# Expert blocks in another order: where the helpers' work for the next block stands, in a one-core Trainium2 kernel

## The chip, the core and the metric

The kernel runs on one core of a Trainium2 chip. The core has five engines with instruction streams of their own, which wait for each other through semaphores: TensorE (PE) multiplies matrices, VectorE (DVE) and ScalarE (ACT) work elementwise and can read TensorE's results in PSUM, GpSimd (POOL) works elementwise and issues gathers and scatters, SyncE (SP) issues other DMAs. The metric is the device time of one execution in microseconds; the figure for the kernel is the median of three runs.

## What is computed

Six sublayers stand one after another, each of the form x = x + f(layernorm(x)): cross attention, self attention, a feed-forward layer, cross attention again, a recurrent memory, and a mixture of experts. x is 16 x 64 x 256 in float32, the context 16 x 1601 x 192. The change touches the last sublayer alone (1024 tokens of width 256, eight experts, the two best for each token, and a shared expert for all):

```
logits = normed @ router_w.T;  probs = softmax(logits)
top_v, top_i = top_k(probs, 2);  gates = softmax(top_v)
for e in range(8):
    gate, up = split(normed @ gate_up_w[e].T)      # 256 -> 2 x 768
    y = (silu(gate) * up) @ down_w[e].T            # 768 -> 256
    out = out + comb[:, e, None] * y
out = out + swiglu(normed, shared_gate_up_w, shared_down_w)
```

## The kernel before

The program is a list of functions for each sublayer, one per engine, called one after another; what an engine does stands in the order of the calls in the code. In `moe` (L2525) the routing first sorts the 2048 pairs of token and expert into `NS` = 23 blocks of 128 rows, each of one expert. `itu` and `itd` hold, for each block, the offset of its expert's weights in the SBUF tensors `gu` and `dn`.
For block i the work is this:

- GpSimd gathers 128 rows (`gather`, three ahead) into `xs`.
- TensorE transposes them (`turn_block`, two transposes on L166, PSUM bank 6), VectorE scales and shifts them into `XT` (`take_block`, L2773).
- ScalarE rounds `XT` to fp32r as the high part `Xh` (`block_high`, L2947), GpSimd subtracts it to get the low part `Xl` (`block_low`, L3010).
- The expert's gate/up weights come in three thirds f = 0, 1, 2 of 1024 columns in all. ScalarE rounds each to its high part `hi[f]` (`up_high`, L2953), VectorE makes the low part `lo[f]` (`up_low`, L2783).
- TensorE makes the product of each third in PSUM bank f (`gate_up`): four matmuls with the high weights (L2666, L2667), two with the low ones (L2670). Block 0 alone uses float32 weights directly (L2660).
- ScalarE applies silu to one half of the product (L2939), VectorE multiplies it with the other (L2789) into `a_`.
- TensorE transposes the six 128-column pieces of `a_` (`turn_a`, six transposes on L166), ScalarE copies them to SBUF in two copies (L2961), and TensorE makes the down product from them (`down`, L2692; each of its six float32 matmuls appears as two).
- VectorE scales the result by the gates (L2795) and GpSimd adds it to the output rows in HBM (`add`, L3017).

The loop is software pipelined. In the round of block i TensorE does the products of block i, the turns and the down product of block i-1, and the transposes of a later block's input. The weights' parts for block i+1 are made meanwhile, a third at a time, each behind the product of block i that frees its buffer. Every engine works in order, so an instruction that waits holds all that are queued behind it on that engine.

The register load for the down product (L2686) stands on TensorE ahead of all waits of `down`; ScalarE's (L2981) at the start of a round; VectorE's (L2782) in `up_low`, behind its wait for the high part.

Of the kernel before, what the change touches and what calls it, by code (L numbers as in the profile page):

```python
# [16 lines left out]
NS = 23  # L17
# [2507 lines left out]
def moe(c, m, ended, tail):  # L2525
# [32 lines left out]
    ids, itu, itd = m.irest[:, 0:NS], m.irest[0:1, NS:2 * NS], m.irest[0:1, 2 * NS:3 * NS]  # L2558
# [9 lines left out]
    routed, routing, prob = c.sig("routed"), c.sig("routing"), c.sig("prob")  # L2568
# [35 lines left out]
    def pe(e, w):  # L2604
# [36 lines left out]
        def turn_block(i):  # L2641
            w.wait_ge(*in_xs[i % 3](i))
            w.wait_ge(*emptied[6])
            for k in range(2):
                p = c.turn(e, ps[:, 6, 128 * k:128 * k + 128], xs[i % 3][:, 128 * k:128 * k + 128])
            p.then_inc(b_turned.at(i), 1)
            emptied[6] = b_taken(i)

        off = {}
# [33 lines left out]

        def down(i):
            bank = (5, 7)[i % 2]
            off[i, 1] = e.value_load(itd[:, i:i + 1], min_val=0, max_val=7 * 1536)  # L2686
            for part in range(2):
                w.wait_ge(*a_taken((i, 3 + part)))
                w.wait_ge(*in_dn(7))
                w.wait_ge(*emptied[bank])  # L2690
                for f in range(4 * part, 4 + 2 * part):
                    p = e.matmul(ps[:, bank, 0:256], aT[i % 2][:, f, :], dn[:, bass.ds(off[i, 1] + 256 * f, 256)],  # L2692
                                 start=(f == 0), stop=(f == 5))
            p.then_inc(y_made.at(i), 1)
            emptied[bank] = y_out(i)
# [29 lines left out]
            emptied[b] = s  # L2725
        turn_block(0)
        for i in range(NS):
            gate_up(i, 0)
            gate_up(i, 1)
            if i:  # L2730
                turn_a(i - 1)
            else:
                turn_block(1)
            gate_up(i, 2)
            if i + 2 < NS:
                turn_block(i + 2)
            if i:
                down(i - 1)
        turn_a(NS - 1)
# [2 lines left out]
    def dve(e, w):  # L2742
# [34 lines left out]
        off = {}  # L2777

        def up_low(i, f):
            w.wait_ge(*up_hi((i, f)))  # L2780
            if f == 0:
                off[i] = e.value_load(itu[:, i:i + 1], min_val=0, max_val=7 * 3072)  # L2782
            e.tensor_tensor(lo[f], gu[:, bass.ds(off[i] + 1024 * f, 1024)], hi[f], ALU.subtract).then_inc(up_lo.at((i, f)), 1)  # L2783

        def gate_up(i, f):
            w.wait_ge(*silu((i, f)))
            w.wait_ge(*(a_turned((i - 2, 4)) if i >= 2 else sh_down(NT - 1)))
            w.wait_ge(*routed("table"))
            e.tensor_tensor(a_[i % 2][:, 256 * f:256 * f + 256], ps[:, f, 256:512], sg[f], ALU.mult).then_inc(a_made.at((i, f)), 1)  # L2789
# [116 lines left out]
        shared_down(1)  # L2906
        take_block(0)
        for i in range(NS):
            gate_up(i, 0)
            gate_up(i, 1)  # L2910
            if i == 0:
                take_block(1)
            if i + 1 < NS:
                up_low(i + 1, 0)
            gate_up(i, 2)
            if i + 2 < NS:
                take_block(i + 2)
            if i + 1 < NS:
                up_low(i + 1, 1)
            if i:  # L2920
                down(i - 1)
            if i + 1 < NS:
                up_low(i + 1, 2)
        down(NS - 1)

    def act(e, w):
        def shared_act(half, f):
            w.wait_ge(*sh_up((half, f)))
            if half:
                w.wait_ge(*sh_act((half - 1, f)))  # L2930
            e.activation(sgs[f], ps[:, sh_bank(half, f), :], ACT.Silu).then_inc(sh_silu.at((half, f)), 1)

        def gate_up(i, f):
            w.wait_ge(*g_made((i, f)))
            if i:
                w.wait_ge(*a_made((i - 1, f)))
            else:
                w.wait_ge(*sh_down(NT - 1))
            e.activation(sg[f], ps[:, f, 0:256], ACT.Silu).then_inc(silu.at((i, f)), 1)  # L2939

        off = {}

        def block_high(i):
            w.wait_ge(*b_taken(i))
            if i >= 3:
                w.wait_ge(*g_made((i - 2, 2)))
            e.copy(Xh[i % 2], XT[i % 2]).then_inc(x_hi.at(i), 1)  # L2947

        def up_high(i, f):
            if i == 1:  # L2950
                w.wait_ge(*(h_out("h"), routing("down"), sum_out(1))[f])
            w.wait_ge(*g_made((i - 1, f)))
            e.copy(hi[f], gu[:, bass.ds(off[i] + 1024 * f, 1024)]).then_inc(up_hi.at((i, f)), 1)  # L2953

        def turn_a(i):
            for n, b in ((4, 3), (2, 4)):
                f0 = 0 if b == 3 else 4
                w.wait_ge(*a_turned((i, b)))
                if i >= 2:
                    w.wait_ge(*y_made(i - 2))  # L2960
                e.copy(flat(aT[i % 2][:, f0:f0 + n, :]), ps[:, b, 0:128 * n]).then_inc(a_taken.at((i, b)), 1)  # L2961

        e.activation(c.sd[:, 0:1], c.ident[:, 0:1], ACT.Sqrt).then_inc(c.ac.at(), 1)
        tail.take_rows(e, w, LT - 2, 6, 256)
        tail.take_rows(e, w, LT - 1, 6, 0)
        w.wait_ge(*c.dv(("moments", into, LT)))
        w.wait_ge(*c.po("eps"))
        e.activation(c.sd[:, LT:NT], c.mv[:, LT, 1:2], ACT.Sqrt, bias=c.eps).then_inc(c.root.at(into), 1)
        e.activation(c.sd[:, 1:2], c.ident[:, 0:1], ACT.Exp).then_inc(c.ac.at(), 1)
        ended(w)  # L2970
        w.wait_ge(*routing("logits"))
        e.activation(pr, lg, ACT.Exp).then_inc(prob.at("in"), 1)
        w.wait_ge(*routing("gap"))
        e.activation(g2, v2, ACT.Exp).then_inc(prob.at("gate"), 1)
        for half in range(2):
            for f in range(2):
                shared_act(half, f)
        w.wait_ge(*routing("down"))
        for i in range(NS):
            if i + 1 < NS:  # L2980
                off[i + 1] = e.value_load(itu[:, i + 1:i + 2], min_val=0, max_val=7 * 3072)  # L2981
            gate_up(i, 0)
            gate_up(i, 1)
            if i:
                turn_a(i - 1)
            else:
                block_high(1)
            if i + 1 < NS:
                up_high(i + 1, 0)
            gate_up(i, 2)  # L2990
            if i + 1 < NS:
                up_high(i + 1, 1)
            if i + 2 < NS:
                block_high(i + 2)
            if i + 1 < NS:
                up_high(i + 1, 2)
        turn_a(NS - 1)

    def pool(e, w):
        def gather(i):  # L3000
            w.wait_ge(*routing("ids"))
            w.wait_ge(*h_out("h"))
            if i >= 3:
                w.wait_ge(*b_turned(i - 3))
            e.indirect_dma_start(xs[i % 3], None, c.xs_d, bass.IndirectOffsetOnAxis(ap=ids[:, i:i + 1].bitcast(U32), axis=0)
                                 ).then_inc(in_xs[i % 3].at(i, 16), 16)

        def block_low(i):
            w.wait_ge(*x_hi(i))
            e.tensor_tensor(Xl[i % 2], XT[i % 2], Xh[i % 2], ALU.subtract).then_inc(x_lo.at(i), 1)  # L3010

        def add(i):
            w.wait_ge(*y_out(i))
            w.wait_ge(*sum_out(1))
            if i:
                w.wait_ge(*added(i - 1))
            e.indirect_dma_start(rows_out, bass.IndirectOffsetOnAxis(ap=ids[:, i:i + 1].bitcast(U32), axis=0), yS[i % 2], None,  # L3017
                                 bounds_check=1023, oob_is_err=False, compute_op=ALU.add).then_inc(added.at(i, 16), 16)

        root_pool(c, e, w, into, LT - 1)  # L3020
        ended(w)
        e.memset(C_[:, :, NS:NS + 1], 0.0).then_inc(c.po.at("past the last"), 1)
        w.wait_ge(*routing("placed"))
        w.wait_ge(*c.dv("gates"))
        ce = cmp_[:, 0:16 * NS].rearrange("p (i s) -> p i s", s=NS)
        e.tensor_tensor(B[:, :, NS:2 * NS], ce, g12.unsqueeze(2).broadcast_to([128, 16, NS]), ALU.mult).then_inc(gated.at("in"), 1)
        for i in range(3):
            gather(i)
        for i in range(NS):
            if i + 3 < NS:  # L3030
                gather(i + 3)
            if i == 0:
                block_low(1)
            if i + 2 < NS:
                block_low(i + 2)
            if i:
                add(i - 1)
        add(NS - 1)
# [236 lines left out]
```

## Time and profile before

| | |
|---|---|
| median of three runs | 1865.37 us (1861.46 to 1867.23) |
| profiled execution, its own time | 1867.23 us |
| its span | 1865.4 us |
| TensorE busy, share of the span | 1790.0 us, 96% |
| VectorE busy | 1353.5 us, 73% |
| ScalarE busy | 1009.7 us, 54% |
| GpSimd busy | 946.4 us, 51% |
| chain that ended last: TensorE, VectorE, ScalarE | 79%, 9%, 6% |

The loop over the expert blocks fills the last 190 us or so of the span. Two things help in reading the rows further down. Matmuls overlap, so one row's duration is longer than the room it takes; the chain of waits shows that room. And a timeline merges equal instructions that follow each other: `x2` is two of them.

### The profile page before, as it was taken

The numbers are of one execution on the slowest core, as the hardware profiler recorded it, in microseconds if no ns is written. First come the engines' busy times: TensorE is split into PE (matmuls) and PEld (weight loads), VectorE is DVE, ScalarE is ACT, GpSimd is POOL, SyncE is SP. The second block draws the span as 40 slices with busy tenths as digits, with TensorE's granted clock in tenths as the row PEclk, the third lists the DMA queues.
The fourth block names the chain that finished last, engine by engine and source line by source line (L and its number), as shares of the span: only waits on it lengthen the run. The fifth ranks groups of instructions, "written<-read, shape, count | busy, mean of one in ns | idle before, by whom it ended". The sixth has DMA issues, their size and how long they took to land.

```text
span 1865.4 us, 44745 instructions
## 1 busy us (share of the span) xinstructions
PE 1790.0 (96%) x17870; PEld 1558.2 (84%) x17870; DVE 1353.5 (73%) x2786; ACT 1009.7 (54%) x2138; POOL 946.4 (51%) x1205
## 2 busy tenths in 40 slices
PE   6999999999999999999999999999999999999998
PEld 5788887878877778899998999999999986667887
DVE  6888888888888877566766766676666745756775
ACT  3666666766667745454444444444444434526664
POOL 5877777777777617445433334333433313514553
PEclk9999999999999999999999999999999999989999
DMA  5112111112110110044222222222223007051111
GB/s 162 37 44 66 38 38 37 38 53 57 38 37 3 59 50 1 20 122 116 63 62 62 63 62 63 62 63 63 81 70 85 14 2 296 2 192 23 32 31 16
DMA packets 50750, 113.11 MB, mean 61 GB/s; under 512 B 4928, under 2 KB 37264, under 8 KB 49008
## 3 DMA queue, kind: packets, MB, share of 16 engines
q1 hardware_dynamic: 46128, 105.13, 19.0%
q0 software_dynamic: 4416, 5.12, 1.6%
q8 instruction: 143, 2.34, 0.5%
q14 instruction: 63, 0.52, 0.1%
HBM read 105.78 MB, written 5.37 MB: 60 GB/s over the span
## 4 chain that ended last, share of the span: by engine, by line
PE 79%; DVE 9%; ACT 6%; issue 3%; DMA 2%; POOL 0%; SPq 0%; POOLq 0%; DVEq 0%; ACTq 0%
PE ps L104 9%; PE ps L166 8%; PE ps L502 5%; PE ps L483 5%; PE ps L1717 5%; PE ps L460 4%; PE ps L2692 3%; PE ps L477 3%; PE ps L1718 2%; PE ps L412 2%; DVE arena L1829 2%; PE ps L1704 2%; PE ps L1706 2%; PE ps L1703 2%; PE ps L1705 2%
## 5 line engine op out<-in xcount | busy, mean ns | idle before, releaser
L576 DVE TENSOR_REDUCE arena<-ps 128x1 f32<-128x400 f32 (+1 forms) x512 | 257.5, 565 | 82.4 <-PE ps L460 82.1
L731 ACT ACTIVATE arena<-ps 128x384 f32<-128x384 f32 (+1 forms) x512 | 223.3, 524 | 94.4 <-PE ps L483 94.0
L1717 PE MATMUL ps<-arenaR 128*128 128x386 f32 x768 | 242.9, 374 | 1.1 <-DVE arenaR L1823 1.1
L815 POOL TENSOR_TENSOR arena<-arena 128x512 f32<-128x512 f32 (+1 forms) x152 | 196.7, 1294 | 81.6 <-ACT arena L731 74.4
L1933 ACT CAST arenaR<-ps 128x512 fp32r<-128x512 f32 (+1 forms) x256 | 116.8, 509 | 200.4 <-PE ps L166 199.5
L1718 PE MATMUL ps<-arenaR 128*128 128x194 f32 x768 | 194.4, 253 | 0.0
L1823 DVE TENSOR_TENSOR arenaR<-ps,arenaR 128x512 fp32r<-128x512 f32 (+1 forms) x256 | 138.9, 585 | 28.9 <-ACT arenaR L1933 28.9
L1958 ACT ACTIVATE wsb<-ps,arena 128x1200 f32<-128x1200 f32 x64 | 81.0, 1265 | 131.4 <-DVE arena L1882 131.4
L1718 PEld LDWEIGHTS ps<-arenaR 128*128 128x128 f32 x768 | 147.5, 192 | 0.0
L1717 PEld LDWEIGHTS ps<-arenaR 128*128 128x128 f32 x768 | 145.4, 189 | 1.4 <-DVE arenaR L1823 1.4
L1829 DVE TENSOR_REDUCE arena<-ps 128x1 f32<-128x400 f32 (+1 forms) x256 | 137.0, 566 | 0.6 <-PE ps L1707 0.6
L502 PEld LDWEIGHTS ps<-arena 128*32 128x32 f32 (+1 forms) x3328 | 87.0, 110 | 42.6 <-ACT arena L731 42.4
L1973 POOL TENSOR_TENSOR arenaR<-wsb,arenaR 128x400 fp32r<-128x400 f32 (+1 forms) x32 | 28.7, 898 | 182.8 <-ACT arenaR L1905 182.7
L1973 POOL TENSOR_TENSOR xA<-wsb,xA 128x400 fp32r<-128x400 f32 (+1 forms) x32 | 29.3, 916 | 170.8 <-ACT xA L1905 170.5
L166 PE MATMUL ps<-ident,wsb 128*128 128x128 f32 (+1 forms) x832 | 112.2, 273 | 3.2 <-ACT wsb L1960 2.2
L483 PE MATMUL ps<-arena 32*128 32x128 f32 x3328 | 114.3, 269 | 0.0
L2783 DVE TENSOR_TENSOR ring<-gu,ring 128x1024 fp32r<-128x1024 f32 x66 | 81.7, 1238 | 44.3 <-ACT ring L2953 41.7
L483 PEld LDWEIGHTS ps<-arena 32*128 32x128 f32 x3328 | 112.5, 186 | 1.2
L460 PE MATMUL ps<-arena 32*128 32x400 f32 (+1 forms) x1024 | 111.8, 499 | 0.3 <-DVE arena L570 0.3
L502 PE MATMUL ps<-arena 128*32 128x128 f32 (+1 forms) x3328 | 104.2, 274 | 3.9 <-ACT arena L731 0.4
L605 DVE TENSOR_TENSOR arena<-arena 128x512 f32<-128x512 f32 x132 | 104.4, 791 | 1.4
L166 PEld LDWEIGHTS ps<-ident,wsb 128*128 128x128 f32 (+1 forms) x832 | 98.1, 140 | 7.2 <-ACT wsb L1960 2.4
(384 smaller groups left out, 5116.8 us busy)
## 6 DMA issues: line engine op xcount, KB each, us to landing
wsb<-in_ctx SPq DMA_DIRECT2D x16, 1152.0 KB
wsb<-in_ctxT SPq DMA_DIRECT2D x16, 800.5 KB, 5.2
wsb<-in_ctxT SPq DMA_DIRECT2D x32, 400.2 KB, 7.5
gu<-in_m_gu SPq DMA_DIRECT2D x8, 1536.0 KB, 19.2
arena<-in_ctxT SPq DMA_DIRECT2D x15, 800.5 KB, 5.2
arena<-in_ctxT SPq DMA_DIRECT2D x30, 400.2 KB, 7.2
dn<-in_m_dn SPq DMA_DIRECT2D x8, 768.0 KB, 11.4
wsb<-in_f_w SPq DMA_DIRECT2D x2, 1024.0 KB, 5.9
```

The lines of the kernel that those rows point to most:

```text
L104: m = e.matmul(out, a, b, start=(first and i == 0), stop=(last and i == n - 1))
L166: return e.transpose(out, v, self.ident[0:k, 0:k])
L460: e.matmul(ps[:, bk, 0:real], flat(qd[n % 3])[r, :], K[n % 2][r, k.start:k.start + real], start=True, stop=True).then_inc(seen.at((n, i)), 1)
L483: a = e.matmul(ps[:, use[u], 128 * t:128 * t + 128], K[n % 2][r, k], flat(qd[n % 3])[r, :], start=False, stop=(t == T - 1))
L502: a = e.matmul(ps[32 * u:32 * u + 32, bk, 0:128], V[b % 2][0:rows, k, f + 32 * u:f + 32 * u + 32], probs(n, s)[0:rows, u, 128 * t:128 * t ...
L576: e.tensor_reduce(mx4[n % 2][:, u, i:i + 1], ps[:, at("look", n, i, u), 0:400 + (i == 3)], AX.X, ALU.max).then_inc(c.maxed.at((n, i, u)), 1)
L731: e.activation(v[:, u, 0:128 * GN[s]], ps[:, at("st", n, s, u), 0:128 * GN[s]], ACT.Exp).then_inc(c.exp_a.at((x0, n, s, u)), 1)
L815: e.tensor_tensor(sums_p[0:k], sums_p[0:k], v[0:k, :, 128 * t:128 * t + 128], ALU.add).then_inc(added_p.at((n, s)), 1)
L1717: e.matmul(o, PTh[:, t, :], v[:, t, 0:386], start=(t == 0), stop=False)
L1718: e.matmul(o[:, 0:194], PTl[:, t, :], v[:, t, 0:194], start=False, stop=False)
L1823: e.tensor_tensor(lo, ps[0:k, 4 + g % 2, 0:u], hi, ALU.subtract).then_inc(c.p_lo.at((x1, n, g)), 1)
L1829: e.tensor_reduce(mx4[n % 2][:, i:i + 1], ps[:, i, 0:400 + (i == 3)], AX.X, ALU.max).then_inc(c.dv.at(), 1)
```

## The change

Five things are moved, all within the loop over the blocks.

- The input of block i+1 (`turn_block`, `take_block`, `block_high`, `block_low`) is prepared at the start of round i, where before the input of block i+2 was prepared late in round i. On ScalarE it stands behind the first silu.
- ScalarE casts the high part of third f right behind the silu of third f; before, thirds 0 and 1 came one place later. The copies of `turn_a` stand ahead of the second cast.
- VectorE makes the low part of third f right behind the multiply of third f.
- VectorE scales the down product behind all three low parts.
- The register load of `down` stands behind the waits of its first part, and ScalarE's stands in `up_high`, behind its wait.

```diff
         def down(i):
             bank = (5, 7)[i % 2]
-            off[i, 1] = e.value_load(itd[:, i:i + 1], min_val=0, max_val=7 * 1536)
             for part in range(2):
                 w.wait_ge(*a_taken((i, 3 + part)))
                 w.wait_ge(*in_dn(7))
                 w.wait_ge(*emptied[bank])
+                if part == 0:
+                    off[i, 1] = e.value_load(itd[:, i:i + 1], min_val=0, max_val=7 * 1536)
                 for f in range(4 * part, 4 + 2 * part):
...
@@ pe
         for i in range(NS):
+            if 0 < i < NS - 1:
+                turn_block(i + 1)
             gate_up(i, 0)
             gate_up(i, 1)
...
             gate_up(i, 2)
-            if i + 2 < NS:
-                turn_block(i + 2)
             if i:
                 down(i - 1)
...
@@ dve
         for i in range(NS):
+            if 0 < i < NS - 1:
+                take_block(i + 1)
             gate_up(i, 0)
+            if i + 1 < NS:
+                up_low(i + 1, 0)
             gate_up(i, 1)
             if i == 0:
                 take_block(1)
             if i + 1 < NS:
-                up_low(i + 1, 0)
+                up_low(i + 1, 1)
             gate_up(i, 2)
-            if i + 2 < NS:
-                take_block(i + 2)
             if i + 1 < NS:
-                up_low(i + 1, 1)
+                up_low(i + 1, 2)
             if i:
                 down(i - 1)
-            if i + 1 < NS:
-                up_low(i + 1, 2)
...
@@ act, up_high
             w.wait_ge(*g_made((i - 1, f)))
+            if f == 0:
+                off[i] = e.value_load(itu[:, i:i + 1], min_val=0, max_val=7 * 3072)
             e.copy(hi[f], gu[:, bass.ds(off[i] + 1024 * f, 1024)]).then_inc(up_hi.at((i, f)), 1)
...
@@ act
-        w.wait_ge(*routing("down"))
         for i in range(NS):
+            gate_up(i, 0)
+            if 0 < i < NS - 1:
+                block_high(i + 1)
             if i + 1 < NS:
-                off[i + 1] = e.value_load(itu[:, i + 1:i + 2], min_val=0, max_val=7 * 3072)
-            gate_up(i, 0)
+                up_high(i + 1, 0)
             gate_up(i, 1)
             if i:
                 turn_a(i - 1)
             else:
                 block_high(1)
             if i + 1 < NS:
-                up_high(i + 1, 0)
+                up_high(i + 1, 1)
             gate_up(i, 2)
-            if i + 1 < NS:
-                up_high(i + 1, 1)
-            if i + 2 < NS:
-                block_high(i + 2)
             if i + 1 < NS:
                 up_high(i + 1, 2)
...
@@ pool
-            if i == 0:
-                block_low(1)
-            if i + 2 < NS:
-                block_low(i + 2)
+            if i + 1 < NS:
+                block_low(i + 1)
             if i:
                 add(i - 1)
```

On TensorE, from the third product of a block to the first matmul of the down product, before (L166 are the input transposes, `s_a_taken` counts ScalarE's copies):

```order
L2666 MATMUL ps<-ring,xr 128x512 [waits s_up_hi]
L2667 MATMUL ps<-ring,xr 128x512
L2666 MATMUL ps<-ring,xr 128x512
L2667 MATMUL ps<-ring,xr 128x512
L2670 MATMUL ps<-ring,xr 128x512 [waits s_up_lo]
L2670 MATMUL ps<-ring,xr 128x512
L166 MATMUL ps<-ident,rest 128x128 [waits s_b_taken,s_in_xs1]
L166 MATMUL ps<-ident,rest 128x128
L2686 TENSOR_LOAD irest
L2686 ISA x2
L2692 ISA [waits s_routing,s_a_taken]
L2692 MATMUL ps<-dn,rest 128x256
```

The same place now:

```order
L2666 MATMUL ps<-ring,xr 128x512 [waits s_up_hi]
L2667 MATMUL ps<-ring,xr 128x512
L2666 MATMUL ps<-ring,xr 128x512
L2667 MATMUL ps<-ring,xr 128x512
L2670 MATMUL ps<-ring,xr 128x512 [waits s_up_lo]
L2670 MATMUL ps<-ring,xr 128x512
L2691 TENSOR_LOAD irest [waits s_routing,s_a_taken]
L2691 ISA x2
L2693 ISA
L2693 MATMUL ps<-dn,rest 128x256
```

The input transposes now follow the down product, and the wait for the copies stands on the register load instead of behind it.

On ScalarE, one round before (L2939 silu, L2961 copies of the turned activations, L2953 cast of a weight third, L2947 cast of an input block):

```order
L2981 TENSOR_LOAD irest
L2981 ISA x2
L2939 ACTIVATE rest<-ps 128x256 [waits s_a_made,s_g_made] x2
L2961 COPY rest<-ps 128x512 [waits s_a_turned]
L2961 COPY rest<-ps 128x256 [waits s_a_turned]
L2953 ISA
L2953 COPY ring<-gu 128x1024
L2939 ACTIVATE rest<-ps 128x256 [waits s_a_made,s_g_made]
L2953 ISA
L2953 COPY ring<-gu 128x1024
L2947 CAST xr<-rest 128x256 [waits s_b_taken]
L2953 ISA
```

And now, up to the copies of the turned activations:

```order
L2940 ACTIVATE rest<-ps 128x256 [waits s_a_made,s_g_made]
L2948 CAST xr<-rest 128x256 [waits s_b_taken]
L2955 TENSOR_LOAD irest
L2955 ISA x2
L2956 ISA
L2956 COPY ring<-gu 128x1024
L2940 ACTIVATE rest<-ps 128x256 [waits s_a_made,s_g_made]
L2964 COPY rest<-ps 128x512 [waits s_a_turned]
L2964 COPY rest<-ps 128x256 [waits s_a_turned]
```

The two silu that stood together are parted by the input cast, the register load and a weight cast, and the copies come behind all of them.

## Rows read from the trace of the kernel before

**Rows 1.** Busy time by stretch: length, each engine (instructions), granted clock, DMA share, GB/s.

```profile
1675.00:1694.34 19.34, 15.18 (x55) 10.04 (x55) 9.20 (x17) 8.38 (x15) 4.62 (x4) 0.91 0.14 44
1694.34:1840.00 145.66, 145.66 (x727) 122.95 (x726) 108.23 (x174) 95.93 (x171) 76.76 (x56) 1.00 0.18 31
```

**Rows 2.** Chain of waits (start us, us, what): down of block 0, one block, the end.

```profile
1692.10 2.59 PE ps L2692 x12
...
1725.29 0.23 PE ps L2666
...
1728.06 0.66 PE ps L166 x6
...
1730.10 0.22 PE ps L166 x2
1730.32 2.59 PE ps L2692 x12
1732.91 0.23 PE ps L2666
...
1854.91 0.59 ACT rest L2961
```

**Rows 3.** Timeline, head of the loop: start us, us, what, [idle before <-releaser].

```profile
1677.25 3.70 PE L2660 MATMUL ps<-gu,rest 128*128 x8 [2.55 <-issue]
1679.26 0.38 ACT L2939 ACTIVATE rest<-ps 128x256 f32<-128x256 f32 x1 [12.87 <-PE ps L2660]
1683.94 0.47 PE L2666 MATMUL ps<-ring,xr 128*128 128x512 f32 x1 [0.84 <-ACT ring L2953]
1686.16 1.16 PE L2670 MATMUL ps<-ring,xr 128*128 128x512 f32 x2 [1.07 <-DVE ring L2783]
```

**Rows 4.** Timeline of TensorE and ScalarE, one block, and the last down product.

```profile
1721.65 1.06 ACT L2953 CAST ring<-gu 128x1024 fp32r x1
...
1727.89 0.82 PE L166 MATMUL ps<-ident,rest 128*128 128x128 f32 x6
1728.09 0.39 ACT L2939 ACTIVATE rest<-ps 128x256 f32<-128x256 f32 x1 [0.75 <-PE ps L2670]
...
1728.53 0.86 ACT L2961 COPY rest<-ps 128x512 f32<-128x512 f32 x2
...
1729.27 1.06 ACT L2953 CAST ring<-gu 128x1024 fp32r x1
...
1730.15 2.75 PE L2692 MATMUL ps<-dn,rest 128*128 x12
1730.22 0.40 ACT L2939 ACTIVATE rest<-ps 128x256 f32<-128x256 f32 x1
1730.50 1.05 ACT L2953 CAST ring<-gu 128x1024 fp32r x1
...
1855.63 2.85 PE L2692 MATMUL ps<-dn,rest 128*128 x12 [0.54 <-ACT rest L2961]
```

**Rows 5.** Register loads by line: ns min/median/max, first and last start us.

```profile
L2658 PEldq TENSOR_LOAD <-irest x1: 809/809/809, 1675.9 to 1675.9; - x1
L2686 PEldq TENSOR_LOAD <-irest x23: 297/301/315, 1690.1 to 1852.8; - x23
L2981 ACTq TENSOR_LOAD <-irest x22: 273/279/480, 1666.5 to 1840.3; - x22
```

**Rows 6.** Timeline of VectorE, where it makes a first low part.

```profile
1723.47 1.23 DVE L2783 TENSOR_TENSOR ring<-gu,ring 128x1024 fp32r<-128x1024 f32 x1 [1.48 <-ACT ring L2953]
1724.62 0.42 DVE L2789 TENSOR_TENSOR rest<-ps,rest 128x256 f32<-128x256 f32 x1
1724.95 0.72 DVE L2773 TENSOR_SCALAR rest<-ps,small 128x128 f32<-128x128 f32 x2
...
1731.30 1.23 DVE L2783 TENSOR_TENSOR ring<-gu,ring 128x1024 fp32r<-128x1024 f32 x1 [2.15 <-ACT ring L2953]
```

## The prediction, made before the changed kernel was run

> **What bounds the kernel now.** I began with the windows of the loop over the 23 expert blocks, the only place that the change touches. From 1694.34 to 1840.00 us, about nineteen blocks, TensorE is busy for 145.66 of 145.66 us at a granted clock of 1.00, while VectorE, ScalarE and GpSimd are busy for 108.23, 95.93 and 76.76 us; ahead of it (1675.00 to 1694.34) TensorE is busy for 15.18 of 19.34 us at a clock of 0.91 [rows 1]. "Busy" alone would not prove that TensorE is the limit, so the chain of waits comes next: one block runs from 1725.29 to 1732.91 us, 7.62 us, and is made of TensorE pieces alone. The first two gate/up products take 2.77 us (to 1728.06), the six transposes of the previous block's activations 0.66, the third product 1.39, the two transposes of a new input block 0.22, the down product 2.59 [rows 2]. They sum to 7.63. There is no gap to win. The reader is to see that in this stretch a reordering can only keep 7.62 us or add to it, and that time can be won only before 1694 us, and there is little: 4.16 us of idle TensorE [rows 1], of which the waits for the first fp32r weights are 0.84 (ScalarE's high part) and 1.07 us (VectorE's low part) [rows 3].
>
> Then the timelines of the helpers, for how late each could be. ScalarE's activation of a product starts 0.20 us after the product leaves the array (1728.09 against the transposes' start at 1727.89), its copy of the turned activations 0.64 us after the turns begin (1728.53) [rows 4]. The down product starts at 1730.15, so the copy, 0.59 us long [rows 2, 4], has been done for a full microsecond. That microsecond is the cover which the change spends.
>
> **The change, part by part.** I count time in a block from t, where the two input transposes start, which in the new order stand ahead of the block. By the pieces above the products leave the array at t+1.61, 3.00 and (after the turns, at 3.66) 5.04; the down product is due at 5.04, the next block at 7.63.
>
> *Transposes moved from behind the third product to the head of the block.* The same two matmuls per block, 0.22 us either way, between neighbours that show no gap [rows 2]: nothing gained, nothing lost. The gathers that fill their input are issued by GpSimd in the same order. The transposes are no longer between the third product and the down product.
>
> *ScalarE.* Now, behind the first activation, stand the cast of the next input block, a register load, and the 1.06 us cast of the first weight third; the second activation and the copy of the turned activations are queued behind these. First activation at t+1.81. The input cast needs VectorE's taken block, which I put at t+1.3 to 1.8, just in time. The register load takes 0.28 us by itself [rows 5]; with the register steps behind it I take 0.7 from the activation's start (VectorE's shortest, from the end of what it waited for to its next operation, is 0.76: 1721.65 + 1.06 to 1723.47 [rows 4, 6]). The weight cast starts at t+2.5, the second activation 0.95 behind it (1729.27 to 1730.22 [rows 4]) at 3.45, later than the 3.20 at which its product allows it, and the copy 0.28 later (1730.22 to 1730.50 [rows 4]) at 3.73, where TensorE would have allowed 3.64. So the copy ends at 3.73 + 0.59 = t+4.32.
>
> *TensorE's register load for the down product.* Before, it stands ahead of every wait and costs 0.30 us [rows 5] while the array still works off queued matmuls. Now it carries the wait for that copy, and the six matmuls are queued behind it. The trace of before shows no such load on TensorE in the flow, so I bound it. VectorE has exactly this form, a load that waits for ScalarE and an operation that uses it: 0.76 us (above) or 0.97 us (1729.27 + 1.06 to 1731.30) [rows 4, 6]. A wait without a load costs 0.13 us on TensorE (1854.91 + 0.59 to 1855.63) [rows 2, 4]. The only load on TensorE that had just been released took 0.81 us, with 1.35 us from its start at 1675.9 to the matmul at 1677.25 [rows 3, 5]. The low end is 0.13, if the load were somehow done ahead of its wait; the high end is 1.35. I take 0.76 to 0.97, the nearest form that occurs in the flow, since every first load of an engine is longer than its later ones (ScalarE 0.48 once against a median of 0.28 [rows 5]). Then the down product starts at t + 4.32 + 0.76 to 0.97 = 5.08 to 5.29, and 0.10 more for an array that starts from rest (its twelve matmuls took 2.85 us so, 2.75 in the flow [rows 4]). Against 5.04 that is a gap of 0.14 to 0.35 us; I take 0.25. The matmuls queued ahead cover nothing of this, since they are what ends at 5.04.
>
> The Trainium skill, Perfetto Trace Analysis, section Per-engine timelines, says that a matmul's wait stands in a queue beside the sequencer, while an instruction of the sequencer itself first waits and then executes. By that rule the load cannot begin before the copy has ended and its whole cost lies behind the wait, a gap of 0.14 to 0.35; if the load could run ahead, the sum would be that of the first rival below. VectorE's 0.76 and 0.97 us agree with the rule.
>
> *VectorE and GpSimd.* VectorE takes the input block first and makes each low part right behind the gate multiply of its third. The work is the same, so its 108 of 146 us don't bind; but its order closes a loop with ScalarE: weight cast 1.06, load behind it 0.76 to 0.97, low part 1.15, multiply 0.33, low part 1.15, multiply 0.33, low part 1.15, gate scale (priced as the multiply of equal size) 0.33, input block 0.72 [rows 4, 6], then input cast and load on ScalarE, 0.7. That is 7.7 to 7.9 us, against the 7.62 of TensorE. It would set the same period as the gap does, 7.76 to 7.97, so the two are not added. GpSimd's subtract comes a place earlier, its result is due a block later; nothing.
>
> *Head.* The first high part can be cast at about 1679.9, straight behind the activation at 1679.26 [rows 3], instead of behind the input block. But on VectorE the block-1 input now stands behind the first low part: cast end 1680.95, + 0.97, + 1.15, multiply 0.33, input 0.72, ends near 1684.15; cast and subtract take it to 1685.5 to 1686. Block 1's first product then starts 1.6 to 2 us later than 1683.94 but doesn't pause for its low part, so it ends where it did. The down product of block 0 waits through input block 2, its cast, the load, a weight cast and the copy to about 1692.4; it was at 1692.10 [rows 2]. Head: +0.3.
>
> *End.* The last down product directly ends the program and is waited for: 0.13 becomes 0.76 to 0.97, +0.7.
>
> Sum: 0.3 + 20 blocks x 0.25 + 0.7 = +6.0 us. The profiled execution took 1867.2 us around its span of 1865.4 and was the slowest of the three; it would become 1873.2. On the median, 1865.4, the forecast is 1871.4.
>
> **The rivals.** (1) *No gap; not slower.* The point from which it decides is t+5.04: if copy end plus load come to less, because the load is under 0.7 us or ScalarE's cast starts before t+2.4, the period stays 7.62. For it: the margin is a tenth or two. Against: the loop over VectorE needs 7.7 as well. Price: 0.3 + 0.7, time 1866.4. (2) *The load behind a wait costs on TensorE what its one row shows*, 1.35 instead of 0.87: gap 0.73, 20 x 0.73 + 0.3 + 1.2 = +16.1, time 1881.5. Against it: that load was TensorE's first of the loop. (3) *The head wins.* The early cast takes away the waits of 0.84 and 1.07 and with them the stretch of lower clock (at 0.91 over 19.34 us, 1.7 us), nothing is lost later but the 0.7 at the end: time 1862.5. Against: the input block of block 1, which it needs too, is later.
>
> **How the numbers follow.** Forecast 0.50, rival 1 0.27, rival 2 0.13, rival 3 0.06, and 0.04 for something slower still. A measurement of this kernel tells 0.3%, 5.6 us, from no change. The forecast's own range is 0.3 + 20 x 0.14 + 0.6 to 0.3 + 20 x 0.35 + 0.9, +3.7 to +8.2, of which two thirds lie above 5.6. So slower 0.33 + 0.13 + 0.04 = 0.50, faster half of rival 3 and some of the scatter, 0.04, the same 0.46. The range reaches to both rivals: 1864 to 1881.
>
> **What would show it.** Right: the windows of the loop show TensorE idle for some 3%, 0.1 to 0.4 us just ahead of each down product, with the register load or ScalarE's copy named before it; a block takes 7.76 to 7.97 us; the last down product starts 0.8 to 1 us behind the copy. Wrong: blocks of 7.62 us; or a gap ahead of the gate/up products, which would mean that the input block or the weights are late; or a shorter head.

## The result

| | before | changed |
|---|---|---|
| median | 1863.41 us (4 runs, 1861.42 to 1867.23) | 1880.59 us (4 runs, 1878.49 to 1881.38) |
| ratio of the times | | 1.0111, 95% interval 1.0066 to 1.0156 |
| profiled execution, its span | 1867.23 us, 1865.4 us | 1875.34 us, 1873.5 us |
| TensorE busy in the span | 1790.0 us | 1787.2 us |

The change makes the kernel slower by about 17 us by the medians, 12 to 29 us by the interval. (The two medians alone stand at 1.0092 to each other. The record lists eleven executions of the changed kernel in all, from 1875.34 to 1900.76 us.) The forecast was +6 us, so the sign was right and the size was wrong by a factor of almost three, just inside the far end of the stated range.

The two profiled executions differ by 8.1 us only. The reason lies ahead of the loop, in code that the change doesn't touch. First the kernel before, then the changed one, in the windows view (columns as in [rows 1]):

```profile
1600.00:1675.00 75.00, 69.40 (x390) 49.07 (x388) 50.25 (x184) 28.40 (x94) 25.31 (x85) 0.91 0.29 111
```

```profile
1600.00:1675.00 75.00, 67.00 (x389) 46.21 (x387) 51.09 (x183) 28.05 (x90) 25.49 (x83) 1.00 0.33 120
...
1675.00:1694.34 19.34, 16.53 (x73) 13.20 (x74) 13.43 (x22) 12.47 (x22) 6.79 (x6) 0.91 0.11 21
1694.34:1840.00 145.66, 136.50 (x661) 110.44 (x660) 108.81 (x158) 85.65 (x154) 73.32 (x51) 1.00 0.16 28
```

The clock granted to TensorE in the last 75 us ahead of the loop was 0.91 there and 1.00 here, and the changed kernel's profile enters the loop 7.9 us early (its block 0 starts at 1669.34 us instead of 1677.25). Not all of this is the clock's: the same matmuls, of the sublayer before, were already 2.0 us apart at 1634 us, with the clock at 1.00 in both; the rest came between 1640 and 1660 us, where the clock was 0.74 before and 1.00 now. From the start of block 0 to the end the profiles say 188.1 us before and 204.2 us now, 16 us more, which is close to the difference of the medians. So everything below compares stretches inside the loop. In the long one TensorE has fallen from 145.66 [rows 1] to 136.50 us of 145.66, at a clock of 1.00: it waits for 6% of the time, where the forecast spoke of 3%.

### The profile page after: what moved, and what is told of

Same layout as the page of the kernel before. It is cut to its first block, busy times and chain, and to the rows that moved or that the text cites. A ratio compares the mean times of both kernels' runs of the same rounds, so it can differ in the third digit from the quotient of the medians.

```text
span 1873.5 us, 44745 instructions
## 1 busy us (share of the span) xinstructions
PE 1787.2 (95%) x17870; PEld 1551.3 (83%) x17870; DVE 1363.1 (73%) x2786; ACT 1008.1 (54%) x2138; POOL 946.5 (51%) x1205
## 4 chain that ended last, share of the span: by engine, by line
PE 69%; DVE 13%; ACT 8%; issue 5%; DMA 2%; DVEq 1%; POOL 1%; SPq 0%; ACTq 0%; POOLq 0%
PE ps L104 7%; PE ps L166 7%; PE ps L502 5%; PE ps L1717 5%; PE ps L483 5%; PE ps L460 4%; PE ps L477 2%; PE ps L1718 2%; PE ps L412 2%; DVE arena L1829 2%; DVE arenaR L1823 2%; DVE ring L2784 2%; PE ps L1704 2%; PE ps L1707 2%; PE ps L1703 2%
## 5 line engine op out<-in xcount | busy, mean ns | idle before, releaser
L2784 DVE TENSOR_TENSOR ring<-gu,ring 128x1024 fp32r<-128x1024 f32 x66 | 93.2, 1412 | 48.0 <-ACT ring L2956 43.4
L166 PE MATMUL ps<-ident,wsb 128*128 128x128 f32 (+1 forms) x832 | 112.2, 273 | 4.0 <-ACT wsb L1960 2.2
L166 PEld LDWEIGHTS ps<-ident,wsb 128*128 128x128 f32 (+1 forms) x832 | 98.0, 140 | 8.6 <-DVE arenaR L1823 2.8
```

Of the source, the lines that this page charges most:

```text
L166: return e.transpose(out, v, self.ident[0:k, 0:k])
```

## The profile after: what ends a block

The chain of waits was made of TensorE pieces alone [rows 2]. In the changed kernel, over one whole block, it doesn't touch TensorE at all (start us, us, what; a q behind an engine's name is its sequencer):

```profile
1723.47 1.06 ACT ring L2956
1724.53 0.03 issue
1724.56 0.30 DVEq L2783
...
1725.28 1.31 DVE ring L2784
1726.59 0.38 issue
1726.97 0.41 DVE rest L2790
1727.38 0.43 DVE ring L2784
...
1728.64 0.40 DVE rest L2790
...
1730.11 0.47 DVE rest L2796
1730.58 0.65 DVE rest L2774 x2
1731.25 0.29 ACT xr L2948
...
1731.88 1.06 ACT ring L2956
```

From weight cast to weight cast it is 8.41 us (1723.47 to 1731.88). Read in order of time: ScalarE casts the first weight third, VectorE loads its register and makes the low part, does a gate multiply, the second low part, a multiply, the third low part, the scale of the down product, the next input block; ScalarE casts that input, loads its register and casts again. The prediction had named this loop and priced it at 7.7 to 7.9 us. The timelines of VectorE, GpSimd and TensorE in the same block show where the rest comes from (engine, operation, then the idle time before it):

```profile
1725.28 1.76 DVE L2784 TENSOR_TENSOR ring<-gu,ring 128x1024 fp32r<-128x1024 f32 x1 [2.14 <-ACT ring L2956]
1726.97 0.41 DVE L2790 TENSOR_TENSOR rest<-ps,rest 128x256 f32<-128x256 f32 x1
1727.30 1.42 DVE L2784 TENSOR_TENSOR ring<-gu,ring 128x1024 fp32r<-128x1024 f32 x1
1728.64 0.41 DVE L2790 TENSOR_TENSOR rest<-ps,rest 128x256 f32<-128x256 f32 x1
1728.97 1.21 DVE L2784 TENSOR_TENSOR ring<-gu,ring 128x1024 fp32r<-128x1024 f32 x1
...
1724.88 0.98 POOL L3005 DMA_INDIRECT rest<-h_rows,irest  x1 [0.30 <-issue]
1725.88 1.75 POOL L3010 TENSOR_TENSOR xr<-rest,xr 128x256 fp32r<-128x256 f32 x1
...
1726.12 2.85 PE L2693 MATMUL ps<-dn,rest 128*128 x12 [0.61 <-ACT rest L2964]
...
1734.55 2.85 PE L2693 MATMUL ps<-dn,rest 128*128 x12 [0.56 <-ACT rest L2964]
```

The first low part now takes 1.76 us instead of 1.23 [rows 6], the second 1.42, the third, beside which GpSimd does nothing, still 1.21. GpSimd's subtract for the next input block starts at 1725.88, inside the first of them, and itself takes 1.75 us. In the first two blocks of this trace, where it follows an idle stretch of GpSimd and VectorE is idle too, it takes 0.73. TensorE's gap stands ahead of the down product, just as forecast, and is 0.6 us; but it is the place where TensorE catches up with the loop, not what makes the block long.

## The experiments

All times are medians; the ratio is to the kernel before on the same chip, whose median was 1862.38 to 1864.32 us there, so a ratio can differ a little from the quotient of two times in the table. "Block" is the mean distance of the down products' starts over blocks 2 to 19 of the profile. Theory A: the loop over VectorE and ScalarE sets the block, and the collision with GpSimd's subtract makes up the part of it that the prediction missed. Rival B is the prediction's own main term: TensorE's register load behind its wait.

| kernel | time, us | ratio (95% interval) | block, us |
|---|---|---|---|
| before | 1863.41 | | 7.63 |
| changed | 1880.59 | 1.0111 (1.0066 to 1.0156) | 8.41 |
| changed, TensorE's load ahead | 1877.95 | 1.0070 (1.0049 to 1.0092) | 8.41 |
| changed, scatter-adds later | 1866.93 | 0.9998 (0.9980 to 1.0015) | 7.72 |
| changed, small subtract | 1867.92 | 1.0010 (0.9993 to 1.0027) | 7.73 |
| changed, subtract ahead of gather | 1868.85 | 1.0028 (1.0009 to 1.0047) | 7.73 |
| changed, VectorE's load ahead | 1868.38 | 1.0027 (1.0013 to 1.0041) | 7.82 |
| changed, ScalarE's load ahead | 1870.35 | 1.0030 (1.0016 to 1.0045) | 7.97 |
| before, TensorE's load behind | 1865.86 | 1.0008 (0.9984 to 1.0031) | 7.63 |
| changed, adds later, TensorE's load ahead | 1863.99 | 1.0004 (0.9983 to 1.0025) | 7.67 |
| changed, adds later, all loads ahead | 1862.02 | 0.9995 (0.9981 to 1.0008) | 7.62 |
| the last one with a new head | 1857.37 | 0.9965 (0.9949 to 0.9982) | 7.62 |

(For four of them, at 7.72, 7.73, 7.73 and 7.67, one block of 8.0 us is left out of the mean; with it they are 7.74, 7.74, 7.75 and 7.69. The two means of 7.63 hold one block of 7.72 or 7.67 among blocks of 7.62.)

**TensorE's load back ahead of its waits.**

```diff
         def down(i):
             bank = (5, 7)[i % 2]
+            off[i, 1] = e.value_load(itd[:, i:i + 1], min_val=0, max_val=7 * 1536)
             for part in range(2):
                 ...
-                if part == 0:
-                    off[i, 1] = e.value_load(itd[:, i:i + 1], min_val=0, max_val=7 * 1536)
```

> The changed kernel, but with TensorE's register load for the down product back ahead of its waits. Theory A (a loop of waits over VectorE and ScalarE sets the block's 8.41 us; TensorE's gap ahead of the down product is only where it waits for it): the block stays at 8.4 us, TensorE now idles as long elsewhere or still there behind ScalarE's copy, and only the end gets 0.7 us shorter: about 1 us less than the changed kernel. Rival B (the load behind the wait is what sets it, as the prediction had it): the gap of about 0.75 us closes, the block falls to 7.6 to 7.8 us, 13 us less.

Measured: the block stays at 8.41 us, and TensorE still idles ahead of the down product, now for 0.53 us:

```profile
1728.29 2.85 PE L2692 MATMUL ps<-dn,rest 128*128 x12 [0.53 <-ACT rest L2963]
```

The two last down products are 3.95 us apart as before the change, not 4.71, so what the load does cost is at the end. The first two distances between down products also stayed at 7.62 here (7.76 and 8.44 in the changed kernel), and the loop took over only after them. Rival B falls: removing the suspected cost from each of 20 blocks gives back none of their length.

**Scatter-adds one round later.**

```diff
-            if i:
-                add(i - 1)
+            if i > 1:
+                add(i - 2)
+        add(NS - 2)
         add(NS - 1)
```

> The changed kernel, but GpSimd issues each block's scatter-add one round later, so that its subtract for the next input block runs while VectorE waits for ScalarE, not beside VectorE's first and second low part. Theory A with the collision (the low parts take 1.76 and 1.41 instead of 1.23 us beside the subtract, which takes 1.75 instead of 0.73): low parts back at 1.2, the subtract at 0.75, the block at 7.7 to 7.9 us, 10 to 14 us less than the changed kernel. Rival B: no change to the block.

Measured: 0.9998 of the kernel before, 14 us less than the changed kernel, the block 7.72 us. GpSimd no longer stands in its scatter while the cast input lies ready; it subtracts at once, while VectorE is idle. Rows by line (ns min/median/max), VectorE's low parts and GpSimd's subtract:

```profile
L2784 DVE TENSOR_TENSOR ring<-gu,ring x66: 1211/1215/1226, 1678.6 to 1845.9; 128x1024 fp32r<-128x1024 f32 x66
...
L3010 POOL TENSOR_TENSOR xr<-rest,xr x22: 724/734/742, 1681.3 to 1841.3; 128x256 fp32r<-128x256 f32 x22
```

In the changed kernel the same two are:

```profile
L2784 DVE TENSOR_TENSOR ring<-gu,ring x66: 1207/1410/1781, 1674.3 to 1853.8; 128x1024 fp32r<-128x1024 f32 x66
...
L3010 POOL TENSOR_TENSOR xr<-rest,xr x22: 727/1746/1762, 1677.0 to 1849.5; 128x256 fp32r<-128x256 f32 x22
```

The block is not back at 7.62, and the waits say what sets it now. In the changed kernel ScalarE's input cast waited for VectorE in every block (us in total, times, longest us; 1700 to 1830 us):

```profile
ACT xr L2948 <- DVE rest L2774: 3.7, 15, 0.3
```

With the scatter-adds later no such wait is left in that stretch: ScalarE waits only for TensorE's product, and its first copy ends 0.78 us ahead of the down product (1726.52 + 0.58 to 1727.88). That is the path of the prediction, through TensorE's register load, and it adds 0.10 us to the block.

**A small subtract.**

```diff
-            e.tensor_tensor(Xl[i % 2], XT[i % 2], Xh[i % 2], ALU.subtract)
+            n = 128 if i < 3 else 2
+            e.tensor_tensor(Xl[i % 2][:, :, 0:n], XT[i % 2][:, :, 0:n], Xh[i % 2][:, :, 0:n], ALU.subtract)
```

> The changed kernel, but from block 3 on GpSimd subtracts only the first 2 of every 128 columns of the input's low part (the rest keeps what an earlier block left); all else, the scatters and gathers included, stays where it is. Theory A with the collision from the subtract: the low parts take 1.2 us, the block 7.7 to 7.9 us, 10 to 14 us less than the changed kernel. Rival C (it is the gather's descriptors, written by GpSimd just before, that slow VectorE): the first low part stays at 1.6 us or more and the block above 8.2 us. Rival B: the block stays at 8.4.

Measured: block 7.73 us. Order, gathers and scatters are those of the changed kernel, and a first low part that runs beside both the gather's issue and the small subtract is not slowed:

```profile
1725.92 0.98 POOL L3005 DMA_INDIRECT rest<-h_rows,irest  x1 [0.30 <-issue]
1726.92 0.73 POOL L3011 TENSOR_TENSOR xr<-rest,xr 128x4 fp32r<-128x4 f32 x1
```

```profile
1726.37 1.22 DVE L2784 TENSOR_TENSOR ring<-gu,ring 128x1024 fp32r<-128x1024 f32 x1 [1.60 <-ACT ring L2956]
```

So it is the size of the subtract's operands that matters, not the gather's issue just before it (rival C) and not the mere presence of an instruction.

**The subtract ahead of the gather.** Two calls of GpSimd change places.

```diff
-            if i + 3 < NS:
-                gather(i + 3)
             if i + 1 < NS:
                 block_low(i + 1)
+            if i + 3 < NS:
+                gather(i + 3)
```

> The changed kernel, but in each round GpSimd's subtract stands ahead of its gather instead of behind it. It starts right behind the scatter's issue, about 1.0 to 1.3 us earlier, while VectorE still waits for its register load. Theory A: the overlap with the first low part shrinks from 1.2 to some 0.2 us, the low parts take 1.2 to 1.4 us, the block 7.7 to 7.9 us, 10 to 14 us less than the changed kernel. Rival: any overlap costs the same, block still above 8.2 us.

Measured: block 7.73 us, the low parts at a median of 1.217 us. GpSimd's and VectorE's timelines:

```profile
1726.59 1.31 POOL L3010 TENSOR_TENSOR xr<-rest,xr 128x256 fp32r<-128x256 f32 x1
1728.07 1.90 POOL L3005 DMA_INDIRECT rest<-h_rows,irest  x1 [0.16 <-issue]
```

```profile
1727.87 1.22 DVE L2784 TENSOR_TENSOR ring<-gu,ring 128x1024 fp32r<-128x1024 f32 x1 [1.60 <-ACT ring L2956]
```

The subtract ends (1727.90) as the low part starts. The gather's issue, which then overlaps the first low part and half of the second, does them no harm. One thing does not fit a collision with VectorE: the subtract takes 1.31 us here, not 0.73, though VectorE is idle from 1726.28 to 1727.87. Its row starts while the scatter's (1725.54, 1.59 us) still runs. So a part of the subtract's 1.75 us in the changed kernel may come from GpSimd's own work ahead of it; how much was not tested.

**VectorE's load ahead of its wait, and ScalarE's at the start of the round** (each alone, on the changed kernel).

```diff
         def up_low(i, f):                       # VectorE
-            w.wait_ge(*up_hi((i, f)))
             if f == 0:
                 off[i] = e.value_load(...)
+            w.wait_ge(*up_hi((i, f)))
...
+                off[i + 1] = e.value_load(...)  # ScalarE, ahead of gate_up(i, 0)
```

> The changed kernel, but VectorE's register load stands ahead of the wait for ScalarE's first cast. Theory A (the block is the length of a loop over ScalarE's input cast and first weight cast and VectorE's low parts, multiplies, scale and input block): the 0.76 us between ScalarE's cast and VectorE's low part fall to about 0.15, and the block by as much, 8.41 to 7.8 us, some 12 us less than the changed kernel, if the subtract collides as before. Rival (the collision alone decides, and it only moves with the low part): the block stays above 8.2 us.

> The changed kernel, but ScalarE's register load stands at the start of the round, as before the change, not between its input cast and its first weight cast. Theory A: the 0.63 us from the start of the input cast to that of the weight cast fall to 0.35, and the block by 0.25 to 0.3 us, to about 8.15 us, 5 to 6 us less than the changed kernel. Rival: no change.

Measured: 7.82 and 7.97 us. The first is 8.41 - 0.6, as the loop predicts, but the agreement is luck, since two more things changed. The collision became milder: the low parts take 1.23, 1.28 and 1.41 us, 0.47 less in sum than in the changed kernel, so the loop by itself would have fallen further. And the loop is no longer what sets the block. TensorE shows next to no gap, and ScalarE's input cast starts right behind its first activation, without a wait for VectorE:

```profile
1700.00:1830.00 130.00, 129.88 (x632) 105.75 (x631) 99.79 (x151) 81.16 (x149) 84.83 (x50) 1.00 0.18 31
```

```profile
1728.90 0.38 ACT L2940 ACTIVATE rest<-ps 128x256 f32<-128x256 f32 x1 [2.90 <-PE ps L2670]
1729.18 0.40 ACT L2948 CAST xr<-rest 128x256 fp32r<-128x256 f32 x1
1729.57 1.05 ACT L2956 CAST ring<-gu 128x1024 fp32r x1
```

ScalarE's first copy ends at 1723.57, and the down product starts 0.83 us later, at 1724.40: the path of the prediction again, through TensorE's load, and 0.20 us on the block. (The row of the matmuls is longer than the room that they take, so a gap of this size hardly shows in the busy time.) The second was to be worth 0.25 to 0.3 and was worth 0.44 and about 10 us instead of 5 or 6. It also moved the collision: blocks of 7.7 to 7.9 and of 8.1 to 8.3 us follow each other, and the median low part is back at 1.226 us with the longest at 1.875. Both runs show that the load which they move was on what set the 8.41 us; the first bounds its worth from below only, and the size of the second was not foreseen.

**The kernel before with TensorE's load behind its waits.** The change's edit of `down`, alone.

> The kernel before, with one edit: TensorE's register load for the down product stands behind the waits of its first part. Theory A: ScalarE's copy is done early enough in the old order (copy end about 0.4 us + 0.76 us ahead of the down product's due time), blocks stay at 7.62 us, only the last two down products start later: +1 us, the same time. Rival B: the load costs 0.3 us or more in each block, +6 to +15 us.

Measured: blocks of 7.62 us, a ratio of 1.0008 (0.9984 to 1.0031), TensorE without a gap:

```profile
1700.00:1830.00 130.00, 130.00 (x649) 109.74 (x649) 96.72 (x155) 86.14 (x155) 69.82 (x52) 1.00 0.18 31
```

In the old order the load's cover, ScalarE's early copy, is there, and the last two down products are 4.66 us apart instead of 3.95. The edit by itself costs 0.7 us.

**Adds later with TensorE's load ahead.**

> The changed kernel with the scatter-adds one round later (no collision) and TensorE's register load ahead of its waits; the loads of VectorE and ScalarE stay where the change put them. With the loads as they were the block was 7.72 us. Theory A': with the collision gone the loop over VectorE and ScalarE is just under TensorE's 7.62 us, and the 0.10 us is TensorE's register load behind its wait: blocks of 7.62 us, and 0.7 us less at the end, 3 us less than with the adds alone. Rival: the loop itself is 7.72 us: the block stays.

Measured: mostly 7.63 to 7.70 us, 7.67 in the mean, between the two theories. So moving TensorE's load gives back about half of the 0.10 us that were left with the collision gone. Then ScalarE's input cast waits for VectorE again (17 times from 1700 to 1830 us, 4.0 us in all): the loop over the helpers takes over at about 7.67. The times (1863.99 against 1866.93) can't tell the two apart.

**All loads ahead, adds later, and then a new head.** With the three loads ahead and the adds later the reordered loop runs as fast as the old one. The last kernel adds this for block 0 alone:

```diff
+        w.wait_ge(*routing("down"))
+        off[0, 0] = e.value_load(itu[:, 0:1], ...)      # TensorE, ahead of the first transposes
         turn_block(0)
         for i in range(NS):
             ...
             gate_up(i, 0)
+            if i == 0:
+                turn_block(1)      # take_block(1) on VectorE: ahead of up_low(1, 0)
             gate_up(i, 1)          # block_high(1) on ScalarE: behind up_high(1, 0)
-            if i == 0: turn_block(1)
```

> The changed kernel with all three register loads ahead of their waits and the scatter-adds one round later (no collision). Theory A: the loop is near 7.0 us and no longer the bound; TensorE has no gap, blocks of 7.62 us; end as before the change. Time 1863 to 1866 us, the same as the kernel before. If a gap of 0.1 us ahead of the down product stays, it isn't the load that makes it.

> The kernel of the run beside it (loads ahead, adds later) with a new head: TensorE's register load for block 0 stands ahead of the input transposes; the transposes of block 1 follow the first product of block 0, VectorE takes that input ahead of the first low part, ScalarE casts it right behind the first weight cast. TensorE should not wait for block 1's operands (0.84 and 1.07 us before), lose about 1.2 us less to the load, and perhaps escape the stretch of half clock: 3 to 5 us less than the kernel before, 1860 us. If the clock falls in any case, 2 to 3 us less.

Measured: 0.9995 (0.9981 to 1.0008) and 0.9965 (0.9949 to 0.9982). The first is the time of the kernel before, as expected; the second beats both kernels, by about 6 us against the one before, a little more than expected. Its TensorE in the head:

```profile
1666.87 0.44 PE L166 MATMUL ps<-ident,rest 128*128 128x128 f32 x2 [0.53 <-DMA rest<-h_rows,irest]
1668.22 1.98 PE L2658 MATMUL ps<-gu,rest 128*128 x4 [0.90 <-DVE rest L2773]
...
1673.83 0.48 PE L2664 MATMUL ps<-ring,xr 128*128 128x512 f32 x1
...
1679.50 2.85 PE L2690 MATMUL ps<-dn,rest 128*128 x12 [0.63 <-ACT rest L2961]
```

Ahead of block 0's first product 0.90 us of idle time instead of 2.55, none ahead of block 1's weights instead of 0.84 and 1.07 [rows 3], and the granted clock stays at 1.00 from 1658 to 1820 us, where it had been 0.91 [rows 1]. From the first transposes to the first down product it takes 12.6 us; before it was 17.6 (1674.31 to 1691.93). How much of this is the clock and how much the waits, the runs don't separate.

## Why the prediction was wrong

*What bounds the kernel now: right.* 7.62 us of TensorE without a gap. No kernel here has a shorter block over blocks 2 to 19, and the one that gained did so in the head.

*TensorE's register load: the mechanism was there, but in the changed kernel it does not set the block.* The load behind the wait took 0.35 us at the median (0.30 to 0.38), and at the end its chain was as forecast. The last down product starts 0.80 us behind the copy (forecast 0.76 to 0.97, before 0.13; TensorE's load itself starts at 1863.0, where the chain names a row of ScalarE's queue):

```profile
1862.40 0.58 ACT rest L2964
1862.98 0.28 ACTq L3047
1863.27 0.51 issue
1863.78 2.87 PE ps L2693 x12
```

In the blocks it was to make 0.14 to 0.35 us each. Where the loop over VectorE is shorter it is what sets the block, at 0.10 us (adds later) and 0.20 us (VectorE's load ahead). In the changed kernel it makes nothing, because TensorE waits for the loop anyway.

*The step that failed* is "GpSimd's subtract comes a place earlier, its result is due a block later; nothing", with the price of the loop, 7.7 to 7.9 us, that follows from it. The term that stood at zero is worth 0.73 us a block: the way from the first low part to the multiply behind it 1.69 us instead of 1.15 (1725.28 to 1726.97), the second 1.34 instead of 1.15 (1727.30 to 1728.64). I had asked when the subtract's result is needed and not what it runs beside. Its new place makes it wait in GpSimd's queue behind a scatter that in turn waits for VectorE's scale, now the last thing in VectorE's round; so it starts inside the first low part of the next round, 0.60 us behind its start. The gap of 20 blocks x 0.25 us was to be 5.0 us; 20 blocks, from the down product of block 0 to that of block 20, became 14.5 us longer (152.35 to 166.86). Without the collision the loop's own price was right: 8.41 - 0.73 is 7.68 us.

Why a GpSimd instruction slows a VectorE one is argued, not shown; what is shown is that the slowdown goes when the subtract is moved or made small.

The Trainium skill, SBUF — State Buffer, section Who interferes with whom, says that a VectorE instruction with two SBUF inputs contends with a GpSimd instruction that reads SBUF; the same page, section SBUF: two separate sides, says that the one that starts first gets the shared pair of ports for its whole length. The low part reads `gu` and `hi` and the gate multiply reads PSUM and one SBUF tile, so the rule picks the right victims: the low parts are slow (1.76 and 1.42 us against 1.21), the multiply at 1726.97, all of it beside the subtract, keeps its 0.41. The kernel before fits the rule of the first start too. VectorE, then GpSimd:

```profile
1725.59 1.21 DVE L2783 TENSOR_TENSOR ring<-gu,ring 128x1024 fp32r<-128x1024 f32 x1
...
1727.20 1.29 DVE L2783 TENSOR_TENSOR ring<-gu,ring 128x1024 fp32r<-128x1024 f32 x1
```

```profile
1726.19 1.22 POOL L3010 TENSOR_TENSOR xr<-rest,xr 128x256 fp32r<-128x256 f32 x1 [2.11 <-ACT xr L2947]
```

The low part that started first keeps its 1.21 us and the subtract takes 1.22 instead of 0.73. Where the rule doesn't fit is the changed kernel: there too the low part started first, by 0.60 us, and yet it took 1.76 us. The spans of GpSimd's instructions are rough, so which of the two really started first is not certain.

*The rivals.* Rival 1 (no gap, 7.62 us) is what the kernel does once the loads stand ahead and the subtract is out of the way. Rival 2 (the load costs 1.35 us) gave nearly the right time, 1881.5, for a wrong reason: the register load on TensorE took at most 0.38 us, and with what follows it 0.80 to 0.84, not 1.35. Rival 3's gain in the head is real, but not in this change: its head took 15.4 us from the first product to the first down product against 14.7 before, +0.7 where I had forecast +0.3. The early cast was there, and block 1's input, which it needs too, was late, as argued against it. The end cost 0.8 us, forecast 0.7. In the recorded chances, +3.7 to +8.2 us was said to lie above 5.6 for two thirds; it is 58%.

*What stays open:* why the subtract of the old order does almost no harm. It overlaps the second low part by 0.6 us and the third by 0.2, and these take 1.21 and 1.29 us; in the changed order, just as far into the first low part but right behind a gather's issue, it costs both. How much of its own 1.75 us is due to GpSimd's issue ahead of it. And why ScalarE's load ahead makes the collision come and go from block to block. None of this was tried further.

## What to carry to other kernels

In a loop that is full on one engine, moving the helpers' work can win nothing in the steady state, so price such a change by the closed loops it makes among the helpers: follow from one instruction back to the same one in the next round, and allow for a collision in every VectorE piece that reads two SBUF tensors while GpSimd may run such a subtract. For each instruction moved ask not only when its result is due but beside what it will start, which is set by the last thing that its queue waits for. A `value_load` is best ahead of the wait, where it cost nothing here. Behind a wait it costs what nothing else covers: nothing in the blocks of the old order, 0.05 us of the block with the adds later, 0.7 us at the end, and at least 0.6 us of the loop on VectorE. And when the piece that sets the time is taken away, look again at what sets it now before reading the gain as that piece's price.

## What the runs showed that I had not expected

- GpSimd's subtract of 128x256 takes 0.73 us where both engines were idle, but 1.31 us beside the end of GpSimd's own scatter, with VectorE idle. One of 128x4 is recorded with 0.73 us too, and doesn't slow VectorE: by these rough spans the length hardly depends on the data, and the collision does.
- Beside it VectorE's 128x1024 subtraction rises from 1.21 to as much as 1.88 us, while gathers and scatters being issued by GpSimd (0.98 to 1.9 us each) leave it at 1.22.
- Two executions of the same code ahead of the loop differed by 8 us, half of the effect to be explained, about 6 of them in a stretch where the granted clock was 0.74 in one and 1.00 in the other. The stretch inside the loop had to be compared by itself.
